# First context tile loaded in halves, later loads held behind it and behind the second task's rows, and the last expert task written outside the loops

## The reference

```python
q, k, v = query @ Wq + bq, key @ Wk + bk, value @ Wv + bv      # head width 32
scores = layer_norm_scores(q @ k.T / sqrt(512))                 # normalised over the 722 keys
head = softmax(scores + mask_term) @ v
x = x + tanh(g_xattn) * (tile(head, 16) @ Wout + bout)          # query = layernorm(x), key = value = ctx

probs = softmax(layernorm(x) @ router_w.T)                      # 8 experts
weights, indices = top_k(probs, 2)
gate, up = split(xn @ w13[e])                                   # w13: 8 x 512 x 2048
y = (silu(gate) * up) @ w2[e]                                   # w2: 8 x 1024 x 512
x = x + tanh(g_ffn) * sum over the two experts of weight * y
```

## Time and profile before

| what | value |
|---|---|
| median of 3 runs | 389.95 us (384.43 to 390.16) |
| profiled execution, its own time | 389.81 us |
| its span in the trace, first to last instruction | 388.2 us |
| PE busy | 360.6 us, 93% of the span |
| DVE, ACT, POOL busy | 263.0, 222.2, 168.2 us |
| DMA | 96.98 MB, mean 250 GB/s |

### The profile page before, as it was taken

How to read it: one execution, slowest core, us unless ns; L and a number is a source line. 1 busy time by engine, 2 the same in 40 slices (tenths; PEclk the granted TensorE clock), 3 DMA queues, 4 the chain that set the end, 5 groups by cost and what they waited for, 6 DMA issues and landing times.

```text
span 388.2 us, 7890 instructions
## 1 busy us (share of the span) xinstructions
PE 360.6 (93%) x2524; PEld 295.4 (76%) x2524; DVE 263.0 (68%) x492; ACT 222.2 (57%) x345; POOL 168.2 (43%) x250
## 2 busy tenths in 40 slices
PE   3799899978968999999999999999999999999992
PEld 3345454567746998999899899989989987777771
DVE  3243968757963997567567657747755773999896
ACT  1123446646633785466456545655565556888884
POOL 3144787886251561750460181055118106443541
PEclk9999989987897999999999999999999999999998
DMA  7999999612479999686786686578667667999960
GB/s 258 346 344 321 345 316 374 256 55 61 105 279 370 367 345 365 217 224 202 227 242 213 209 215 217 200 210 226 218 219 196 210 216 227 255 372 345 410 208 9
DMA packets 21596, 96.98 MB, mean 250 GB/s; under 512 B 5262, under 2 KB 6513, under 8 KB 12106
## 3 DMA queue, kind: packets, MB, share of 16 engines
q1 hardware_dynamic: 14426, 85.71, 63.0%
q0 software_dynamic: 5392, 7.78, 10.1%
q10 hardware_dynamic: 1760, 3.28, 2.5%
HBM read 90.07 MB, written 7.58 MB: 252 GB/s over the span
## 4 chain that ended last, share of the span: by engine, by line
PE 70%; DMA 9%; POOL 8%; issue 5%; DVE 4%; SPq 1%; ACT 1%; ACTq 1%; DVEq 0%; POOLq 0%
PE turnA L580 15%; PE turnB L580 15%; PE scp L594 9%; PE kvp L594 9%; PE scp L542 5%; PE turnB L520 4%; PE turnA L520 4%; DMA stage<-in_wout_dram 4%; DMA xg<-xn_d,ent_next 2%; DMA ent_next<-lists_d 2%; POOL lists_d L1281 2%; DVE w2l L995 1%; PE scp L505 1%; DMA lists_d<-entry,place 1%; DVE w13l L995 1%
## 5 line engine op out<-in xcount | busy, mean ns | idle before, releaser
L995 DVE TENSOR_TENSOR w13l<-stage,w13h 128x1024 fp32r<-128x1024 f32 x88 | 105.6, 1220 | 21.6 <-ACT w13h L705 21.6
L705 ACT ACTIVATE w13h<-stage 128x1024 fp32r<-128x1024 f32 x88 | 90.4, 1052 | 2.9 <-DMA stage<-in_w_dram 2.9
L995 DVE TENSOR_TENSOR w2l<-stage,w2h 128x2048 fp32r<-128x2048 f32 x22 | 50.4, 2294 | 29.0 <-ACT w2h L705 29.0
L1369 POOL DMA_INDIRECT xg<-xn_d,ent_next x10 | 13.5, 1345 | 96.2 <-issue 85.2
L580 PE MATMUL turnA<-xTh,w13h 128*128 128x240 f32 x192 | 52.9, 276 | 0.6 <-DVE h_t L1147 0.6
L580 PE MATMUL turnB<-xTl,w13h 128*128 128x240 f32 x192 | 53.0, 276 | 0.0
L580 PE MATMUL turnA<-xTl,w13h 128*128 128x240 f32 x192 | 52.9, 275 | 0.0
L580 PE MATMUL turnB<-xTh,w13l 128*128 128x240 f32 x192 | 52.9, 275 | 0.0
L580 PE MATMUL turnB<-xTh,w13h 128*128 128x240 f32 x192 | 52.8, 275 | 0.0
L580 PE MATMUL turnA<-xTh,w13l 128*128 128x240 f32 x192 | 52.8, 275 | 0.0
L705 ACT ACTIVATE w2h<-stage 128x2048 fp32r<-128x2048 f32 x22 | 41.8, 1907 | 0.0
(11 more groups left out here) (237 smaller groups left out, 812.9 us busy)
## 6 DMA issues: line engine op xcount, KB each, us to landing
stage<-in_w_dram SPq DMA_DIRECT2D x66, 1024.0 KB, 7.1
ctx_t<-in_ctx_dram SPq DMA_DIRECT2D x8, 1444.0 KB, 16.4
xT_t<-in_xT_dram SPq DMA_DIRECT2D x8, 200.0 KB, 16.4
xn<-in_x_dram SPq DMA_DIRECT2D x8, 200.0 KB
xn_d<-xn ACTq DMA_DIRECT2D x8, 200.0 KB
stage<-in_wout_dram SPq DMA_DIRECT2D x1, 1024.0 KB, 16.2
out_dram<-x ACTq DMA_DIRECT2D x4, 200.0 KB
out_dram<-yw ACTq DMA_DIRECT2D x2, 200.0 KB
```

Source lines behind the costliest of these rows:

```text
L705: act.activation(dst, src, ACT.Copy).then_inc(S["w_hi"], 1)
L995: dve.tensor_tensor(lo, raw, hi.bitcast(F32), ALU.subtract).then_inc(S["w_lo"], 1)
L1369: pool.indirect_dma_start(xg_k[k], None, xn2_d, bass.IndirectOffsetOnAxis(ent_next[:, k, 2:3], 0)).then_inc(S[f"gathered{k}"], 16)
```

## The change

Four edits. **SP at the start**: the tile of the first context batch comes as two DMAs (`load_first_ctx`), the first half ahead of the first rows of x; the load of the second context tile waits for the first half to have landed, and the third x tile now stands behind it. **PE at the start**: `project(0)` waits for each half of its own, and the transpose of the first query stands behind the projection and no longer ahead of it. **SP ahead of task 1**: quarters 1 to 3 and the two halves wait for both gathers of task 1's rows (`gathered0`, `gathered1`), where they waited for the list (`list_in`); one of two register loads moves behind quarter 0. **The last single** is written out behind the loops on PE, ACT and DVE, without the transposes of the next rows and without the splits of the next weights; the loads of those weights fall away, since the bound of SP's loop is lower by one.

```diff
@@ task_ends
-            return (eng.value_load(bounds[0:1, n:n + 1], min_val=2, max_val=TILES - 1) for n in range(2))
+            return (eng.value_load(bounds[0:1, n:n + 1], min_val=2, max_val=TILES - 1) for n in (0, 2))
@@ sync
+            def load_first_ctx(half):
+                part = slice(half * HC // 2, (half + 1) * HC // 2)
+                sp.dma_start(ctx_t[0][:, part, :], ctx_in[0][:, part, :]).then_inc(S[("ctx_first", "ctx_in0")[half]], 16)
...
             load_xT(0)
+            load_first_ctx(0)
             load_x(0)
+            load_first_ctx(1)
             sp.dma_start(mask_u[:], mask).then_inc(S["mask_in"], 16)
-            load_ctx(0)
             load_x(1)
             load_xT(1)
+            sp.wait_ge(S["ctx_first"], 16)
+            load_ctx(1)
             load_x(2)
-            load_ctx(1)
...
             sp.wait_ge(S["tiles_ready"], 1)
-            loads_end = sp.value_load(bounds[0:1, 2:3], min_val=2, max_val=TILES - 1)
             quarter, half = weights_of(1)
             quarter(0)
-            sp.wait_ge(S["list_in"], 16)
+            loads_end = sp.value_load(bounds[0:1, 1:2], min_val=2, max_val=TILES - 1)
+            for k in range(2):
+                sp.wait_ge(S[f"gathered{k}"], 16)
             for q in range(1, NQ):
                 quarter(q)
@@ tensor
             def project(b):
-                pe.wait_ge(*ring("ctx_in", NC, b))
+                if b > 0:
+                    pe.wait_ge(*ring("ctx_in", NC, b))
                 for c in range(HC):
+                    if b == 0 and c == 0:
+                        pe.wait_ge(S["ctx_first"], 16)
+                    if b == 0 and c == HC // 2:
+                        pe.wait_ge(S["ctx_in0"], 16)
...
                     project(i)
+                if i == 0:
+                    turn_query(0)
...
-                if live(i + 1):
+                if live(i + 1) and i >= 0:
                     turn_query(i + 1)
...
-            def single(t, pair_next):
+            def single(t, pair_next, ends=False):
...
-                turn_x(t + 1, 0, 1 if pair_next else 2)
+                if not ends:
+                    turn_x(t + 1, 0, 1 if pair_next else 2)
...
-            pairs_end, tasks_end = task_ends(pe)
+            pairs_end, last = task_ends(pe)
...
-            with pe.Fori(pairs_end, tasks_end) as t:
+            with pe.Fori(pairs_end, last) as t:
                 single(t, False)
+            single(last, False, True)
@@ scalar
-            with act.Fori(pairs_end, tasks_end) as t:
+            with act.Fori(pairs_end, last) as t:
                 single(t)
+            for q in range(NQ - 1):
+                silu(last, q)
+            for q in range(2):
+                h_hi(last, q)
+            silu(last, NQ - 1)
+            for q in range(2, NQ):
+                h_hi(last, q)
+            y_out(last, 0, 4, 2)
@@ vector
-            dve.scalar_tensor_tensor(out=bounds[0:1, 2:3], in0=cums[0:1, 3:4], scalar=3.0, in1=cums[0:1, 2:3], op0=ALU.max, op1=ALU.add
-                                     ).then_inc(S["tabs_made"], 1)
+            dve.wait_ge(S["tabs_made"], 2)
+            dve.tensor_scalar(bounds[0:1, 2:3], bounds[0:1, 1:2], -1.0, None, ALU.add).then_inc(S["tabs_made"], 1)
...
-            with dve.Fori(pairs_end, tasks_end) as t:
+            with dve.Fori(pairs_end, last) as t:
                 single(t)
+            for q in range(NQ - 1):
+                h_mul(last, q)
+            for q in range(2):
+                h_lo(last, q)
+            h_mul(last, NQ - 1)
+            for q in range(2, NQ):
+                h_lo(last, q)
@@ gpsimd
             add_unit(tasks_end, 0, "last_added")
+            pool.wait_ge(S["gathered0"], 16 * tasks_end)
+            pool.wait_ge(S["list_in"], 16 * tasks_end + 16)
             pool.wait_ge(S["last_added"], 16)
```

More of the change, by code:

```diff
@@ L192, in gated_block @@
         yw_k = [yw[0:U, :], yw_b[:]]
-        names = """x_in0 x_in1 x_in2 x_in3 x_in4 x_in5 x_in6 x_in7 xT_in0 xT_in1 xT_in2 ctx_in0 ctx_in1 ctx_in2 small_in wout_in bout_in mask_in
+        names = """x_in0 x_in1 x_in2 x_in3 x_in4 x_in5 x_in6 x_in7 xT_in0 xT_in1 xT_in2 ctx_first ctx_in0 ctx_in1 ctx_in2 small_in wout_in bout_in mask_in
         lists_set lists_put0 lists_put1 out_put0 out_put1 out_put2 out_put3 xn2_put weights_put lists_sent
@@ L854, in _ @@
             first_single()
-            pairs_end, tasks_end = task_ends(act)
+            pairs_end, last = task_ends(act)
             with act.Fori(1, pairs_end) as t:
                 pair(t)
-            with act.Fori(pairs_end, tasks_end) as t:
+            with act.Fori(pairs_end, last) as t:
                 single(t)
+            for q in range(NQ - 1):
[6 more added lines that the diff above has]
+            y_out(last, 0, 4, 2)
         @block.vector
@@ L1216, in _ @@
             first_single()
-            pairs_end, tasks_end = task_ends(dve)
+            pairs_end, last = task_ends(dve)
             with dve.Fori(1, pairs_end) as t:
                 pair(t)
-            with dve.Fori(pairs_end, tasks_end) as t:
+            with dve.Fori(pairs_end, last) as t:
                 single(t)
+            for q in range(NQ - 1):
[5 more added lines that the diff above has]
+                h_lo(last, q)
         @block.gpsimd
```

## The result

The changed kernel is **about 1% slower**: median 390.61 us (388.89 to 392.28, 4 runs) beside 390.06 (384.43 to 390.90, 4 runs) of the kernel before on the same chip, ratio 1.0099, 95% interval [1.0053, 1.0145]. The two medians lie only 0.14% apart: three of the four executions of the kernel before are near 390 us and one is at 384.43. So few executions don't carry the 1% by themselves. The forecast was 389.0 us, 0.8 us faster than before. The measured median lies inside its range, but the change has the wrong sign.

A forecast was written before the change was run, and what follows sets the result against it. PE was taken to bound the kernel from r = 4 on, its restart set by DVE's h_t. Span 388.2 + 0 - 0.35 - 0.4 = 387.4 us, with 1.6 around it 389.0; range 385.6 to 391.6.

The forecast's parts named there:

- What bounds the kernel: PE from r = 4 to the end, 244.50 us at full clock; its 5.15 us xg stall counts only through ACT's late start.
- The hold, -0.35 us: SP ahead of task 1: PE restarts 2.4 us earlier, less 2.05 us of half clock; includes the list's 0.4.
- The half clock: PE behind the new stall at r = 4: 4.1 us at half clock, costing 2.05 us that nothing hides.
- The upper bound of +1.7: Hold's worst case: half of the +4 us that loads at 3.5 us each, not 2.5, would cost.
- The list and quarter 0, -0.4 us: SP before task 1: quarter 0 issued 0.8 us earlier by moving a register load; half of that gained by the list.
- The start, 0 us: Up to Wout: earlier work only lengthens PE's wait for Wout; 0 us, bounds -1.0 to +2.4.
- the dry queue of the rival: Start's hold leaves the load queue dry, Wout up to 2.4 us later, 391.4 us; chance 0.2 shared with slower loads.
- The end, -0.4 us: Last single: dropping four unused transposes saves 0.41 us on PE; bounds -1.0 to +1.0.
- The base: Whole kernel: profiled execution at 389.81 us set equal to the median of 389.95.
- the kept clock: Rival at PE's new stall: clock stays up or returns at once, 387.0 us; chance 0.14.
- the slow gathers: Rival in task 1: row gathers slow for reasons other than weight loads, SP waits for them, 395.2 us; chance 0.06.
- loads slower than 2.5 us: Case for task 1's weight loads after the hold: each takes over 2.5 us; chance 0.2 shared with a late start.

The follow-up runs named there:

- hold_only: Kernel before with one edit: SP waits for both gathers of task 1's rows, not the list, ahead of quarter 1; ratio 1.0106.
- spread_no_hold: Changed kernel with the first pair's weight splits spread over its parts on ACT and DVE, and SP waiting for the list, not the gathers; ratio 1.0006.
- no_hold: Changed kernel with SP waiting for the list again instead of both gathers of task 1's rows; ratio 1.0105 against the kernel before.
- end_only: Kernel before with only the last single written out behind the loops, its unused loads gone, and one register load behind quarter 0; ratio 1.0009.
- warm: Changed kernel with 24 unused products on PE between task 0 and the first pair; ratio 1.0074 against the kernel before.
- after_again: Changed kernel as it is, timed again beside the kernel before; median 388.78 us, ratio 1.0099.
- before_again: Kernel before, unchanged, timed against itself as a control; ratio 0.9984.

## Why the prediction was wrong

- **What bounds the kernel**: right. PE from r = 4 to the end sets the time, at full clock; the wait for xg counts only through DVE's h_t. `hold_only` and `spread_no_hold` both show it: with the wait for xg taken away and DVE's order left, nothing is won, and with DVE's order changed and the wait left, 0.6 us from g (270.6 against 271.2 in `no_hold`). Only both together give 7 us.
- **The hold, -0.35 us**: the step that failed. The forecast let PE restart 25.0 us behind g (134.1 - 109.1), 2.1 us earlier than before, which was to pay for the half clock. It restarted at 28.3 and 28.4 in the two traces of the change and at 27.3 in `hold_only`, where the kernel before has 27.1 and 26.9. So nothing was gained, and the half clock came on top. From g to E the hold was forecast at +0.05 us (the 0.4 of the list lies ahead of g), and it measured +3.0 in `hold_only` (274.5 against 271.4 and 271.6) and +3.4 in the change (274.1 and 274.7 against 271.2 and 270.9 in `no_hold` and `end_only`). The path in it was right link by link, two sizes were not. In the trace of the change quarter 1 is issued 6.1 us after g (111.39 - 105.26) and not 5.4, because xg_b landed at 111.3, 4.6 us after its issue, not 3.9. It lands 4.96 us later, as said. The four loads behind it take 12.5 us, **3.1 us each and not the 2.5** taken from two halves in the earlier trace rows. From the last landing to PE's restart it is 4.69 us (133.56 - 128.87), forecast 4.7. So 0.7 + 2.5 = 3.2 us stand in these two terms. In `hold_only` they are 0.8 and 1.5.
- **The half clock**: right in kind and nearly in size, 2.3 us in the change (half of the 4.7 us at 0.50) and 2.6 in `hold_only` (247.2 - 244.6) beside 2.05; `warm` shows it by taking it away.
- **Why the loads came at 3.1 us**: not because the engines were slow. Between the landings of quarter 1 and of the last half the DMA engines moved 5.15 MB in the change and 4.73 MB in `hold_only`, both at a mean of 411 GB/s (rows below), close to the 422 GB/s of the earlier trace rows. Four loads of 1.05 MB are 4.19 MB, and at 411 GB/s they would take 2.55 us each. The rest, 0.96 and 0.54 MB, is other data. The only other large loads issued by then are the weights of task 2, from 115.11 us on in the change; the gathers of the next rows, issued from 127.40 us, had hardly begun. So part of task 2's data moves before the last half has landed, and the prediction had no term for it. This is worked out from sizes and times of issue; no run holds task 2's loads back.

```profile
DMA packets 765, 5.15 MB, mean 411 GB/s; under 512 B 138, under 2 KB 138, under 8 KB 138
...
DMA packets 702, 4.73 MB, mean 411 GB/s; under 512 B 126, under 2 KB 126, under 8 KB 126
```

- **The bound of the loads' pace**: the prediction had in hand a row of 3.5 us for each load while gathers were in flight, and took the pace of the best pair. The upper bound of +1.7 (+2.1 from g) was made of half of that row and is passed by the measured +3.0. The Trainium skill (DMA: Bandwidth & Descriptors, Specifications) gives about 358 GB/s of HBM for one core, 2.9 us for such a load, and the prediction set it aside for the 422 GB/s of the earlier trace rows. The traces agree with setting it aside: 411 GB/s is the mean of 12.5 us, with stretches of 418 and 430. By the page's pace the forecast would have been 1.6 us higher, +1.65 from g and closer to the result, but for a reason that the trace doesn't bear out.
- **The list and quarter 0, -0.4 us**: quarter 0 is issued 1.39 us after weights_d instead of 1.93, but from weights_d to g it is 10.16 us against 10.27. So 0.5 us is won in SP's queue and only 0.1 us reaches g, a miss inside its bounds.
- **The start, 0 us**: unsettled. In the trace of the change Wout's products begin at 20.28, 1.65 us earlier than before, but over all traces they begin at 21.2 with the new loads and 20.6 without, so that head start is chance. The forecast that nothing is gained stands; a cost of 0.8 to 2.7 us (0.2 to 0.7%), for the most part inside the +2.4 of its bound, is likely. It isn't the dry queue of the rival: from 5 to 12 us the DMA engines are busy for at least 0.92 of each microsecond in the trace of the change.
- **The end, -0.4 us**: right, 244.1 against 244.6 in the traces of `end_only` and `no_hold`.
- **The base**: the forecast set the profiled execution equal to the median. It was one of the longer executions of its kernel: 389.81 beside group medians of 385.4 to 388.4 in the five later groups. That the absolute time fell into the range though the difference was wrong is luck.
- **The rivals**: the kept clock and the slow gathers didn't occur (xg landed 3.8 us after its issue). The price that did occur was in my list only as "loads slower than 2.5 us", in one chance with the start.

## What to carry to other kernels

A wait that is taken away from the front of a chain pays only if what stands next in the queue of the engine behind it is ready: look at what ends the *next* stall, and move the work that is not needed there (here the splits of w2 and of the later quarters ahead of the first h_t) before or together with the wait. The same hold cost 3 us in one order of DVE's work and saved 6 in the other. Price a row of transfers by all the bytes that move in that time, those queued behind it included, and not by the best pair; and compare two traces from a mark behind the noisy part, since here the slower kernel had the shorter span.

## What the runs showed of the hardware

In the change the last w2 half landed 15.1 us after its issue, behind four loads of 1 MB; a gather of rows with nothing big beside it landed in 3.5 to 3.8 us (`after_again` and the change), and with the loads in 8.6. The clock came back 4.7 us after the restart in the change, and in `warm`, where PE stood for 2.22 us only, it did not fall. The larger surprise was the attention phase: between executions of one kernel the time differs by some 8 us (383.48 to 391.46 in `before_again`), and over 101 executions of the kernel before (381.3 to 394.7 us) the time goes with the mean granted clock: its correlation with the time spent at half clock, worked out from that mean, is 0.85. Their standard deviation is 2.1 us (0.55%), so by an estimate from it a difference of 0.3% needs some thirty executions of each kernel to stand out.
